# Context attention with a causal mask: the rows of each block in two halves, the lower half against 64 keys

## The reference, cut to what matters

```
queries = rope((q @ Wq.T).reshape(B, Sq, 32, 128).transpose(0, 2, 1, 3))
keys    = rope((k @ Wk.T).reshape(B, Skv, 8, 128)...)      # each repeated for 4 heads
values  = (v @ Wv.T).reshape(B, Skv, 8, 128)...
scores  = einsum('bhqd,bhkd->bhqk', queries, keys) * 128 ** -0.5
scores  = where(tril(ones((128, 128))), scores, finfo.min)
attn    = softmax(scores, axis=-1)
ctx     = einsum('bhqk,bhkd->bhqd', attn, values)
return ctx.transpose(0, 2, 1, 3).reshape(B, Sq, 4096) @ Wd.T
```

## Time and profile before

| | us |
|---|---|
| median of three runs | 2555.91 |
| lowest and highest | 2554.08, 2557.58 |
| the profiled execution, its own time | 2556.09 |
| its span, first to last instruction | 2554.8 |
| PE busy in the span | 2436.9 |
| DVE, ACT, POOL busy | 1671.0, 989.5, 733.7 |

### The profile page before, as it was taken

How to read it: one execution, slowest core, us unless ns; L and a number is a source line. 1 busy time by engine, 2 the same in 40 slices (tenths; PEclk the granted TensorE clock), 3 DMA queues, 4 the chain that set the end, 5 groups by cost and what they waited for, 6 DMA issues and landing times.

```text
span 2554.8 us, 37687 instructions
## 1 busy us (share of the span) xinstructions
PE 2436.9 (95%) x13016; PEld 1542.3 (60%) x13016; DVE 1671.0 (65%) x3133; ACT 989.5 (39%) x3580; POOL 733.7 (29%) x755
## 2 busy tenths in 40 slices
PE   8999999999999798999999999999998999999998
PEld 7865666666655565456666666556664554555554
DVE  3487777777755777677777777565665644445565
ACT  0013444444444366344444434433555412323330
POOL 1037344443322111364344443222221221000002
PEclk9999999999999999999999999999999999999999
DMA  8452233322322266121333222222661020214430
GB/s 177 101 139 73 76 96 99 87 79 79 93 77 83 91 199 200 62 94 60 95 99 98 89 75 79 87 95 86 191 189 61 22 75 30 95 66 153 132 100 33
DMA packets 220382, 249.97 MB, mean 98 GB/s; under 512 B 49792, under 2 KB 165952, under 8 KB 218144
## 3 DMA queue, kind: packets, MB, share of 16 engines
q1 hardware_dynamic: 212128, 218.20, 28.9%
q10 hardware_dynamic: 8064, 29.36, 3.0%
HBM read 161.49 MB, written 85.98 MB: 97 GB/s over the span
## 4 chain that ended last, share of the span: by engine, by line
PE 80%; DVE 11%; ACT 2%; issue 2%; POOL 2%; DMA 2%; SPq 0%; DVEq 0%; ACTq 0%; POOLq 0%
PE banks L752 12%; PE banks L840 12%; PE banks L824 4%; PE banks L902 4%; PE banks L868 3%; PE banks L303 3%; PE banks L720 3%; PE banks L2091 3%; PE banks L733 3%; PE banks L1521 3%; PE banks L2142 3%; PE banks L2431 2%; PE banks L2468 2%; PE banks L2119 2%; PE banks L2161 2%
## 5 line engine op out<-in xcount | busy, mean ns | idle before, releaser
L947 ACT ACTIVATE E_x<-S_x,sm_x 128x128 f32<-128x128 f32 x512 | 199.2, 390 | 304.3 <-DVE sm_x L1121 304.3
L1183 POOL TENSOR_TENSOR QT<-QT,const 128x512 f32<-128x512 f32 x128 | 171.7, 1342 | 427.7 <-DVE turned L1001 427.7
L161 POOL TENSOR_TENSOR norm_spread<-norm_mv,const 128x1 f32<-128x1 f32 x96 | 20.7, 216 | 909.3 <-DVE norm_mv L157 909.3
L752 PE MATMUL banks<-xT,weights 128*128 128x512 f32 x512 | 237.1, 597 | 7.6 <-POOL weights L1178 5.8
L2589 ACT ACTIVATE E_s<-banks,top_s 128x128 f32<-128x128 f32 x512 | 180.0, 379 | 95.8 <-DVE top_s L2696 95.8
L1079 DVE TENSOR_TENSOR x<-banks,x 128x256 f32<-128x256 f32 (+1 forms) x288 | 147.2, 511 | 84.6 <-PE banks L840 78.6
L840 PE MATMUL banks<-weights,OT 128*128 128x256 f32 x768 | 195.1, 384 | 6.3 <-DVE weights L1062 6.3
L840 PEld LDWEIGHTS banks<-weights,OT 128*128 128x128 f32 x768 | 142.8, 191 | 67.9 <-issue 27.9
L954 ACT ACTIVATE OT<-banks 128x512 f32<-128x512 f32 x128 | 76.1, 595 | 258.2 <-PE banks L902 258.2
L1185 POOL TENSOR_TENSOR QT<-QT,turned 128x512 f32<-128x512 f32 x128 | 169.0, 1320 | 10.0
L752 PEld LDWEIGHTS banks<-xT,weights 128*128 128x128 f32 x512 | 95.0, 191 | 116.5 <-issue 105.6
(11 more groups left out here) (320 smaller groups left out, 4908.1 us busy)
## 6 DMA issues: line engine op xcount, KB each, us to landing
scratch_pt<-blocks_x SPq DMA_DIRECT2D x124, 256.0 KB, 2.0
PT<-scratch_pt SPq DMA_DIRECT2D x496, 64.0 KB, 2.0
scratch_latent_pt<-blocks_s ACTq DMA_DIRECT2D x56, 512.0 KB, 3.6
PT_s<-scratch_latent_pt SPq DMA_DIRECT2D x224, 128.0 KB, 3.0
weights<-in_L_xwq SPq DMA_DIRECT2D x64, 256.0 KB, 3.9
weights<-in_L_xwo SPq DMA_DIRECT2D x64, 256.0 KB, 4.3
scratch_latent_pt<-blocks SPq DMA_DIRECT2D x30, 512.0 KB, 2.6
PT<-scratch_latent_pt SPq DMA_DIRECT2D x120, 128.0 KB, 3.0
```

Source lines behind the costliest of these rows:

```text
L752: mm = PE.matmul(to, left[:, k, head], moving, start=name in ("P1", "P2", "P4", "P5") and k == 0, stop=k == 1, skip_group_check=name in (" ...
L947: ins = AC.activation(head_of(e, j, u), scores_of(s, j, u), ACT.Exp, bias=sm[:, 0, j:j + 1], scale=1.0, accum_out=sm[:, 1, j:j + 1])
L1183: PO.tensor_tensor(four(to), four(to), spread(cos128, 4), ALU.mult).then_inc(*pool_step.one())
```

## The change

Stage 1 alone is treated in halves (`halved`), stage 4 stays as it is. Queries lie in QT by sequence, then upper or lower rows, then head, then 64 rows. In this section "upper" means the rows 64 to 127, which see all keys, and "lower" the rows 0 to 63, which see keys 0 to 63 alone. A unit's scores are then two products of the upper rows of two heads with 128 keys, and two products of the lower rows of two heads with 64 keys: 384 columns where 512 were. S, E, the blocks, the scratch and PT have 384 columns. A new constant `causal_parts` holds the mask of the 384 columns; the constants grow by 384 columns (192 KB).

The value product becomes three: the upper rows with all of V (256 columns, bank 5), the lower rows of heads 0 and 1 with the first 64 rows of V (128 columns, bank 5), the lower rows of heads 2 and 3, whose probabilities lie in partitions 64 to 127 (128 columns, bank 4). The last needs the first 64 rows of V in partitions 64 to 127 as well: SP copies them there once a group (`double_low_values`, 256 KB within SBUF). ACT copies the result in three instructions, DVE takes the sums from OT and not from bank 5, and PE no longer waits for these sums ahead of a value product. For the last two units the turned probabilities come from two transposes and two products with the identity of 64 output rows each, which wait for the copy of the unit before.

The core of the diff:

```diff
-                            for h in range(4):
-                                mm = PE.matmul(psum[2 + u % 2][:, rows_of(h)], QT[g % 2][:, h, rows_of(b)], KT[g % 2][:, rows_of(b)], start=True, stop=True)
+                            if halved:
+                                q = QT[g % 2][:, :].rearrange("p (b a n) -> p b a n", b=B, a=2)[:, b, :, :]
+                                for m in range(2):
+                                    PE.matmul(part(psum[2 + u % 2], m), q[:, 1, rows_of(m)], KT[g % 2][:, rows_of(b)], start=True, stop=True)
+                                for m in range(2):
+                                    mm = PE.matmul(part(psum[2 + u % 2], 2 + m), q[:, 0, rows_of(m)], KT[g % 2][:, b * P:b * P + L], start=True, stop=True)
...
+                            if halved:
+                                PE.wait_ge(*x_ot(u))
+                                for m in range(2):
+                                    PE.transpose(psum[4][:, rows_of(m)], part(E[u % 2], m), ident)
+                                for m in range(2):
+                                    mm = PE.matmul(psum[4][m * L:(m + 1) * L, 2 * P:3 * P], part(E[u % 2], 2 + m), ident, start=True, stop=True)
...
-                            if u % 2 == 0 and 2 <= u <= 2 * pairs:
-                                PE.wait_ge(*x_ot_sums(u // 2))
-                            PE.matmul(psum[5][:, :], V[g % 2][:, b, :], turned_rows(u), start=True, stop=True).then_inc(*x_mix.one())
+                            if halved:
+                                if u == 0:
+                                    PE.wait_ge(*x_other_here(8))
+                                if b == 0:
+                                    PE.wait_ge(*x_low_values(g + 1))
+                                PE.matmul(psum[5][:, 0:2 * P], V[g % 2][:, b, :], turned_upper(u), start=True, stop=True)
+                                PE.matmul(psum[5][:, 2 * P:3 * P], V[g % 2][0:L, b, :], turned_lower(u, 0), start=True, stop=True)
+                                PE.matmul(psum[4][:, 0:P], V_low[g % 2][L:P, b, :], turned_lower(u, 1), start=True, stop=True).then_inc(*x_mix.one())
...
+                    def double_low_values(g):
+
+                        SP.wait_ge(*xv_here(2 * (g + 1)))
+                        if g >= 2:
+                            SP.wait_ge(*x_mix(B * (g - 1)))
+                        SP.dma_start(V_low[g % 2][L:P, :, :], V[g % 2][0:L, :, :]).then_inc(*x_low_values.one())
...
-                        AC.activation(OT[u // 2 % 2][:, u % 2, :, :], four(psum[5][:, :]), ACT.Copy).then_inc(*x_ot.one())
+                        o = OT[u // 2 % 2][:, u % 2, :, :]
+                        if halved:
+                            AC.activation(o[:, :, L:P], four(psum[5][:, 0:2 * P]), ACT.Copy)
+                            AC.activation(o[:, 0:2, 0:L], psum[5][:, 2 * P:3 * P].rearrange("p (h c) -> p h c", h=2), ACT.Copy)
+                            AC.activation(o[:, 2:4, 0:L], psum[4][:, 0:P].rearrange("p (h c) -> p h c", h=2), ACT.Copy).then_inc(*x_ot.one())
...
-                        a11, a12, a21, a22 = four(psum[5])[:, 0:2, :], four(psum[5])[:, 2:4, :], o[:, 0, 0:2, :], o[:, 0, 2:4, :]
+                        odd = o[:, 1, :, :] if halved else four(psum[5])
+                        a11, a12, a21, a22 = odd[:, 0:2, :], odd[:, 2:4, :], o[:, 0, 0:2, :], o[:, 0, 2:4, :]
```

More of the change, by code:

```diff
@@ L524, in load_cross @@
                 views["mask"] = a.load("mask")
+            else:
+                views["V_low"] = quarter(a.place(P, B * P), B)
             views["xT_sums"] = [a.place(P, D) for _ in range(3)] + [place_rest(D) for _ in range(2)]
@@ L536, in cross @@
             direct = units - 2
+            halved = stage == 1
+            W = (3 if halved else 4) * P
+            L = P // 2
             with ExitStack() as scope:
-                QT = [sbuf(f"QT{n}_{stage}", [P, 4, T], scope) for n in range(2)]
+                QT = [sbuf(f"QT{n}_{stage}", [P, 4 * T], scope) for n in range(2)]
                 KT = [sbuf(f"KT{n}_{stage}", [P, T], scope) for n in range(2)]
@@ L699, in sp_cross @@
                         store(u)
+                        if halved and b == 0:
+                            double_low_values(g)
                         if b == 2 and g + 2 < G8:
@@ L876, in pe_cross @@
                                 PE.wait_ge(*x_pt(u - direct))
-                            for h in range(4):
-                                mm = PE.transpose(psum[4][:, rows_of(h)], E[u % 2][:, h, :], ident)
+                            if halved:
[4 more added lines that the diff above has]
+                                    mm = PE.matmul(psum[4][m * L:(m + 1) * L, 2 * P:3 * P], part(E[u % 2], 2 + m), ident, start=True, stop=True)
+                            else:
+                                for h in range(4):
+                                    mm = PE.transpose(psum[4][:, rows_of(h)], part(E[u % 2], h), ident)
                             mm.then_inc(*x_pturn.one())
@@ L933, in turned_copy @@
                         AC.wait_ge(*x_mix(u - 1))
-                        AC.activation(PT[u % 2][:, :, :], four(psum[4][:, :]), ACT.Copy).then_inc(*x_pt.one())
+                        AC.activation(PT[u % 2][:, :], psum[4][:, 0:W], ACT.Copy).then_inc(*x_pt.one())
                     AC.wait_ge(*before.added)
@@ L1084, in turn_blocks @@
                             DV.wait_ge(*x_kept[u % 2](u // 2))
[L1085 removed]
+                        DV.transpose(blocks[u % 2][:, :], E[u % 2][:, :]).then_inc(*x_blocks.one())
                     def add_plain(step, part):
```

115 lines of the change are left out of this document (78 added, 37 removed).

## The result

The changed kernel took 2577.58 us in the median of four runs (2570.62 to 2578.96), the kernel before 2554.99 in the same comparison: the ratio is 1.0082, 95% interval 1.0062 to 1.0102. The changed kernel is 0.8% slower, by some 21 us (16 to 26). The forecast was 2564, its range 2552 to 2573. The direction was right, the size was not: the time lies 4.6 us above the range.

A forecast was written before the change was run, and what follows sets the result against it. The stage was taken as bound by what PE must issue. Tiling +8.1, last two units +1.7 and shorter DVE work -1.5 gave +8.3 us on the profiled 2556.09, 2564.4, so a median of 2564; range 2552 to 2573.

The forecast's parts named there:

- scores: PE's score products: weight loads set the pace, so 64 columns gain at most 0.02 us a unit, taken as 0.
- tiling of the value product: Value product on PE: tiling changes at 0.19 us each make the block 1.04 for 0.86 us, +8.1 us in all.
- operand sums from SBUF: DVE's operand sums reading SBUF instead of PSUM: from nothing to 0.1 us more each on three of them.
- shorter DVE work: DVE masks and transposes 384 columns instead of 512, 0.13 us less each; with the operand sums counted, -1.5 us.
- last two units: Transposes of the last two units: +0.4 us each, plus waits of 0.3 to 0.5 for ACT's copy, together +1.7 us.
- What gets shorter: Step on DVE's chain and PE's 13 waits for L1062: ends -3 and +1 us, -1.5 taken.
- 45 paying units: Units where the value product's extra 0.18 us counts; 18 steps before turn 1 and one in the opening cost nothing.
- Rival 5: More of PE's waits vanish than counted, since DVE is 0.3 us a step faster: 2556 to 2560 us; chance 0.10.
- Hidden: Step pricing at nothing the copy of V's rows, the constants' loads, POOL's smaller pieces and ACT's extra 0.2 us a unit.
- the profiled run as the median: Final step: 2564.4 us forecast for the profiled execution, 0.2 above the median, so the median becomes 2564.
- Rival 4: DVE and POOL slower on 64-column pieces or ACT's copies delaying DVE; PE waits 0.1 to 0.2 at 50 places: 2569 to 2574; chance 0.07.
- Rival 1: Lower value products do not share a slot: 0.11 to 0.22 us more on 64 units, 2571 to 2578 us; chance 0.14.

The follow-up runs named there:

- wide scores: Changed kernel with 128 keys moving in the lower halves' scores too, where 64 did: 2574.75 us (changed kernel's repeat 2575.63).
- sums from PSUM: Changed kernel with the operand sums reading PSUM (banks 5 and 4) again, and PE waiting for them: 2562.30 us, ratio 1.0022.
- both costs out: Changed kernel with operand sums read from PSUM and the lower value products on all 128 rows of weights (wrong keys summed): 2558.28 us, ratio 1.0011.
- stage-1 sums alone: Kernel before with the operand sums reading the SBUF copy (OT) in stage 1 only: 2565.56 us, ratio 1.0039.
- sums from SBUF alone: Kernel before with the operand sums reading the SBUF copy (OT) in both context attentions, stages 1 and 4: 2579.15 us, ratio 1.0098.
- lower products on all rows: Changed kernel with the two lower value products on all 128 rows of weights, without change of tiling (wrong keys summed): 2567.27 us, ratio 1.0054.

## Why the prediction was right or wrong

| | forecast | up to unit 8 | unit 8 to 63 | to the end |
|---|---|---|---|---|
| scores (wide scores) | 0 | | 0 | 0 |
| tiling of the value product | +8.1 | +0.46 | +4.82 | -0.05 |
| operand sums from SBUF | within the -1.5 | +3.55 | +8.48 | 0 |
| the rest: shorter DVE work, ACT's copies, last two units | -1.5 and +1.7 | -2.61 | -1.44 | +2.00 |
| sum | +8.3 | +1.40 | +11.86 | +1.95 |

The rows are distances between traces: tiling is the run with the sums from PSUM less the one with both costs out, the sums are the changed kernel less the one with the sums from PSUM, the rest is the run with both costs out less the kernel before. Up to unit 8 the clock is in the figures too, with up to 1.7 us in +3.55 and in -2.61.

**The step that failed** is in "What gets shorter": "the operand sums read SBUF where they read PSUM: from nothing to 0.1 us each on three of them", and with it "if it gets longer by 0.1, they cost 13 x 0.1 = 1". The first sum grew by 0.49 us in the mean, by 1.04 in the five steps where it counts, and TensorE waited for it. It cost 8.5 us in the stretch, and 10 to 13 in all: 10.6 by TensorE's waits and the stretch, 13 by the medians. In the kernel before, the stage-1 sums alone cost 9.5. I priced the operand by its place and looked at no engine beside DVE. The waits were misread too: of the 13 for L1062 ten are 0.3 us each, two are 0.8 and 0.9 and one is 2.7, where I had them all at 0.6. And the second sum grew with the first (L1138 takes 1.37 in the wait shown above, L1060 took 0.66), so that the chain there became 1.74 us longer. The trace before had the warning. Its DVE group L1060, the only sum with both operands in SBUF, has a mean of 512 ns where L1061 of the same size has 421, and one instruction of it is in the longest wait of the stage, in step 6, in order of time before:

```profile
268.42 0.38 DVE L1059 TENSOR_TENSOR weights<-banks,OT 128x256 f32<-128x256 f32 x1
268.84 1.26 DVE L1060 TENSOR_TENSOR OT<-OT 128x256 f32<-128x256 f32 x1
270.14 0.42 DVE L1061 TENSOR_TENSOR weights<-OT,banks 128x256 f32<-128x256 f32 x1
```

The reason for 0.42 and 1.26 in one chain was there to be asked. L1001, which multiplies QT by constants, both in SBUF, showed it on a larger scale: 42 of its 64 instructions took 0.69 us with POOL idle, 22 beside POOL 1.66. The Trainium skill has the rule, in "SBUF — State Buffer", Who interferes with whom: a DVE instruction with two SBUF inputs contends with a GpSimd instruction that reads SBUF, one with at most one SBUF input does not, and of two that contend the one that comes second is blocked until the first has finished. The traces agree: L1137 ended 0.29 us after POOL's instruction, L1059 with one PSUM operand ran through it in 0.39.

**Right: scores.** The forecast of 0 holds (wide scores, 0.1 us of 521).

**Right in price, too high in count: tiling.** 0.17 us a unit was measured for the forecast 0.18, and the block looked as described: 0.10 of draining, two shared slots, 0.95 to the next product. The 45 paying units were the mis-sized term. 39 of them lie in the stretch (55 value products less 16), which would be 39 x 0.17 = 6.6 us, and it grew by 4.8. Unit by unit, 30 of them paid the 0.17. In the six steps 55 to 60 the tiling cost nothing (0.06 us in all): the output product starts 0.10 after ACT's third copy with the tiling and without it. And the five steps 8g + 4, which I had counted as free, gave 0.15 each back. Without the tiling weight loads wait 0.3 us for the sums in each of them; with it TensorE comes later, and these waits are gone. I had let only the waits right behind the value product take the cost up.

**Right in direction, too small: shorter DVE work.** -1.5 was forecast for the stage. With both costs out the traces give -1.44 in the stretch and -2.61 ahead of unit 8, of which up to 1.7 can be clock. The -1.44 is itself a net: the waits for the sums in steps 22 and 46 fell by 0.76 and 0.64, those in five steps 8g by 0.15 each, one for an add in step 56 by 0.38; against them four records of 128 columns take 0.02 a unit more than two of 512, and ACT's copies 0.10 to 0.14 in each of five steps. So that it meets the forecast is in part luck. Rival 5 counted on more, and its kind is borne out; the time of the run with both costs out (+2.8 us, interval -0.8 to +6.1) does not show it.

**Right: the last two units.** +1.95 from the scores of unit 63 to the end, for 1.7. The last three blocks' tiling, 3 x 0.18 in the forecast, does not show: without it the end takes 23.07, with it 23.02. The tail in order of time after, PE:

```profile
815.75 0.41 PE L934 MATMUL banks<-const,E_x 128*128 128x128 f32 x2 [0.33 <-ACT OT L1028]
```

It waits for ACT's three copies (514.94 to 515.66 in another unit, 0.72 us for the forecast 0.7 to 0.9) by 0.33 us, at the lower end of the forecast 0.3 to 0.5. In the run with both costs out it is up to 0.5, so this wait takes the tiling up.

**Hidden: right but for ACT's copies.** Neither the low values' transfer nor the fetches appear among TensorE's waits of the stage. "ACT's extra 0.2 us a unit stands beside 44 of 100 us" put the copies at nothing; in the last group, where an output product follows the scores at once, they hold TensorE up: five steps are 0.10 to 0.14 us longer with both costs out.

**Wrong: the profiled run as the median.** The median was set equal to the profiled run. Before that was true to 0.2 us; the changed kernel's profiled run is 7 us under its median. With the table's sizes, 5.2 for the tiling, 12.0 for the sums and -2.0 for the rest, the forecast's sum would have been +15.2 on the trace: 2571. The rest, up to 2577, goes with the clock: the granted clock is 0.991 in the profiled run and 0.985 to 0.988 in the three others. Why the changed kernel's runs lie at a lower granted clock (0.9877 in the mean of ten, 0.9894 in the runs of the kernel before) stays open. Longer waits of TensorE go with it in some kernels (sums from SBUF alone: 0.9876) and not in others (lower products on all rows, with the same sums: 0.9894), and the runs with both costs out had 0.9879. No run here separates a cause from chance.

**The rivals.** Rival 4, DVE slower and TensorE's waits longer by 0.1 to 0.2 at 50 places, was nearest in kind and had 0.07. Its places were wrong (pieces of 64 columns: the transpose takes 568 ns alone or beside POOL, the mask 554; ACT's copies hold up TensorE in a few steps, not DVE), and its price too low. Rival 1 would have been near in time for the wrong reason; the traces exclude it.

## What to carry to other kernels

Before an operand is moved from PSUM to SBUF to free a bank or a wait, look at which other engine reads SBUF at that moment: here a VectorE instruction with two SBUF operands stood behind GpSimd's, and what it cost was the rest of GpSimd's instruction, up to 1.04 us. In a chain that TensorE waits for, keep one operand in PSUM, or do the SBUF-only instruction a step earlier, where less waits for it. Before a count of places is multiplied by a price, look at what TensorE waits for next in each kind of step: a cost ahead of a wait can vanish in it. When one instruction of a kind takes two or three times as long as its like in the profile, find out why before pricing more of them; and compare changes of a few us by a stretch of the trace at full clock, since two executions of the same kernel lay 7 us apart here with the clock.

## What the runs showed of the hardware

- VectorE's additions of 128 x 256 float32 with both operands in SBUF took 0.38 to 0.43 us with GpSimd idle and, in the kernel after, 0.80 to 1.42 beside its instructions of 128 x 512; with one operand in PSUM 0.38 to 0.43 in both cases. It works in the other direction too: GpSimd's multiplication (L1266) takes 1.27 us alone and took 1.72 at 488.84, beside an SBUF-only instruction of VectorE. What has one SBUF source did not wait: the transpose of 32 x 32 blocks (568 ns), the mask from PSUM (554), the maximum (420).
- Two products on different halves of the rows, writing the same partitions of two banks, start 10 ns apart or less and share their time in full. The block with a change from 128 rows to 64 and back took 1.05 us to where the next weights are loaded, 0.17 more than the same columns on 128 rows and 0.19 more than one product of 512 columns.
- Of four records with 64 moving columns, each with its own weights, the second starts 0.06 us after the first and the others 0.11, as with 128 columns; the 0.05 comes back behind the group (kernel after and wide scores).
- A product that waits for ACT's copy starts 0.10 us after the copy's end (both costs out, six times).
